# Criss-cross attention on one core: GpSimd's second subtractions of a position without their wait for VectorE's low halves

## The chip, the core and the metric

The kernel runs on one core of a Trainium2 chip. The metric is the time on the device of one execution in microseconds (us), lower is better. Before the change it is 3690.41 us, the median of 3 runs (3687.48 to 3691.53).

## The reference

For each of 8 images of 512 channels and 96 x 96 pixels, queries, keys and values are linear maps of the pixel's channels. Every pixel attends to the 96 pixels of its column (its own left out there) and the 96 of its row, with one softmax over both:

```python
q = jnp.einsum('oc,bchw->bohw', Wq, x) + bq[None, :, None, None]      # 64 channels
k = jnp.einsum('oc,bchw->bohw', Wk, x) + bk[None, :, None, None]
v = jnp.einsum('oc,bchw->bohw', Wv, x) + bv[None, :, None, None]      # 512 channels
energy_H = jnp.einsum('bchw,bcgw->bhwg', q, k) - NEG * eye[None, :, None, :]
energy_W = jnp.einsum('bchw,bchv->bhwv', q, k)
att = jax.nn.softmax(jnp.concatenate([energy_H, energy_W], axis=-1), axis=-1)
att_H, att_W = (att[..., :H], att[..., H:])
out_H = jnp.einsum('bcgw,bhwg->bchw', v, att_H)
out_W = jnp.einsum('bchv,bhwv->bchw', v, att_W)
return gamma * (out_H + out_W) + x
```

All is float32.

## The kernel before

The image is cut into 24 chunks (CHUNKS) of 4 rows (384 pixels). The attention weights are applied to x itself, by column and then by row, into Y, and only that sum is multiplied by the values' weights. Products that need more than one pass of TensorE are made with numbers split into a rounded high part and a low part, low = number - high. The high part is ScalarE's, the low part VectorE's or GpSimd's, and three matmuls (high x high, high x low, low x high) are summed in PSUM.

Each batch has a column stage and then a row stage of 24 positions n. In a position of the row stage TensorE

- multiplies the sums of chunk n by the values' weights (`project`, L1134, four groups of 12 matmuls),
- in positions 6 to 17 also makes queries and keys of two chunks of the next image (`project_kq`, L1032) and their row energies (`split_row_energies`, L1054),
- applies the attention to rows of chunk n + 2 (`attend_row`, L1122, four groups of 8 matmuls, in three PSUM banks that are used in turn, so that the fourth group needs the first one's sum moved out).

The next image's chunks in position n are a_now = [2(n - 6), 2(n - 6) + 1]: the first and the second half of the position. Positions 18 to 22 make the column energies instead. This happens in 7 of the 8 batches; in the last there is no next image.

Around the change:

- ScalarE: `round_kq` rounds keys and queries of a chunk (L602 and L603, the second signals kq_evicted). `round_y` makes the high parts of the sums of chunk n + 1 (L650, two halves), right behind the second `round_kq`. `copy_k` (L608) needs GpSimd's first subtraction. `row_exponentials` (L623, four per chunk) needs VectorE's maximum (L808). `round_x` is L579.
- VectorE: `finish` adds bias and input to a projected group (L881). `low_y` makes the low parts of the sums (L772, two halves, each signals y_lo_made). `add_row` takes a group of row sums out of PSUM (L872). `low_x` is L767. `add_energies` sums the energies' parts and takes their maximum (L805 twice, L808). Its order at the position's end is finish(2), finish(3), low_y half 0, add_row 0, low_y half 1, add_row 1, add_energies, add_row 2 and 3.
- GpSimd: `low_kq` makes the low parts of queries (L496) and keys (L499) of a chunk, once in each half of the position; `scale` (L477) multiplies attention weights by the softmax's factors.

Every engine runs its own list in the order in which it is written; semaphores tie the lists together. In positions 6 to 16 GpSimd has, in front of the second `low_kq`, a wait for both low halves of chunk n + 1. In position 17 (A_LAST) it has none.

Of the kernel before, what the change touches and what calls it, by code (L numbers as in the profile page):

```python
# [17 lines left out]
CHUNKS = N // ROWS  # L18
# [23 lines left out]
A_FIRST, A_LAST = 6, 17  # L42
# [4 lines left out]
def a_chunks(n):  # L47
    return [2 * (n - A_FIRST), 2 * (n - A_FIRST) + 1] if A_FIRST <= n <= A_LAST else []


def b_groups(n):
    first = (n - B_FIRST) * B_EACH
    return list(range(first, min(first + B_EACH, CHUNKS))) if B_FIRST <= n <= B_LAST else []
# [8 lines left out]
def criss_cross_attention(nc, x, x_col, x_row, wqk_t, wv_t, bqk, bv, gamma, out):  # L62
# [5 lines left out]
    HALVES = 2  # L68
# [6 lines left out]
    with ctx:  # L75
# [3 lines left out]
        def sem(name):  # L79
            return ctx.enter_context(nc.semaphore(name))  # L80
# [127 lines left out]
        y_hi_made, y_lo_made, y_half_used = sem("y_hi_made"), sem("y_lo_made"), sem("y_half_used")  # L208
# [12 lines left out]
        def past(s, n):  # L221
            return n + START[s]
# [220 lines left out]
        def _(pool):  # L443
# [3 lines left out]
            def gather_k(a, g):  # L447
                if g == 0:
                    pool.wait_ge(kq_evicted, past(kq_evicted, (a + 1) * CHUNKS))
                    pool.wait_ge(kg_zeroed, a + 1)  # L450
                pool.wait_ge(e_summed, past(e_summed, e_no(a, CHUNKS + g - 2)))
                src = KQ[0:CQ, :].rearrange("p (h w) -> p w h", w=N)[:, g * ROWS:(g + 1) * ROWS, :]
                nc.gpsimd.tensor_copy(Kg[0:CQ, g % 2, :].rearrange("p (w h) -> p w h", w=ROWS), src)\
                    .then_inc(k_gathered, 1)

            def zero_kg(a, before=True):
                if before:
                    out_landed(pool, a - 1, KG_SLOT)
                    pool.wait_ge(p_scaled, past(p_scaled, p_no(a - 1, CHUNKS + B_FIRST + 3)))
                nc.gpsimd.memset(Kg[CQ:P, :, :], 0.0).then_inc(kg_zeroed, 1)  # L460
                pool.wait_ge(kg_zeroed, a + 1)

            def mask(a, g):
                pool.wait_ge(e_exped, past(e_exped, e_no(a, CHUNKS + g)))
                at = by_block(E[0:N, g % ERING, :])
                nc.gpsimd.affine_select(out=at, in_=at, compare_op=ALU.not_equal, fill=0.0, base=0,
                                        pattern=[[-BLOCK, BLOCKS], [0, ROWS], [-1, BLOCK]], channel_multiplier=1)\
                    .then_inc(c_masked, 1)

            def scale(b, i):  # L470
                along, n = i // CHUNKS, i % CHUNKS
                if n == 0:
                    pool.wait_ge(f_made, past(f_made, b * 2 + along + 1))
                pool.wait_ge(p_in[p_buffer(i)], past(p_in[p_buffer(i)], 16 * p_loads(b, i)))
                f = F[:, along, :, n * ROWS:(n + 1) * ROWS].unsqueeze(3).to_broadcast((P, BLOCKS, ROWS, BLOCK))
                at = by_block(weights(i))
                nc.gpsimd.tensor_tensor(at, at, f, ALU.mult).then_inc(p_scaled, 1)  # L477
# [7 lines left out]
            def zero_q(a):  # L485
                pool.wait_ge(e_summed, past(e_summed, e_no(a, CHUNKS - 1)))
                nc.gpsimd.memset(Q[CQ:P, 1, :], 0.0).then_inc(q_zeroed, 1)
                pool.wait_ge(q_zeroed, a)

            def low_kq(a, m, last_scaled):  # L490
                pool.wait_ge(p_scaled, past(p_scaled, p_no(a - 1, last_scaled)))
                if m:
                    pool.wait_ge(kq_low_made, past(kq_low_made, split_no(a, m - 1) * 2))
                pool.wait_ge(kq_evicted, past(kq_evicted, a * CHUNKS + m + 1))
                at = slice(m * CP, (m + 1) * CP)
                nc.gpsimd.tensor_tensor(q_split[CQ:P, :], KQ[CQ:P, at], k_split[CQ:P, 0, :].bitcast(F32), ALU.subtract)\  # L496
                    .then_inc(kq_low_made, 1)
                pool.wait_ge(kq_low_made, past(kq_low_made, split_no(a, m) * 2 - 1))
                nc.gpsimd.tensor_tensor(k_split[0:CQ, 1, :], KQ[0:CQ, at], k_split[0:CQ, 0, :].bitcast(F32), ALU.subtract)\  # L499
                    .then_inc(kq_low_made, 1)  # L500

            def row_stage(b, more):
                scale(b, CHUNKS + 3)
                for n in range(CHUNKS):
                    a_now = a_chunks(n) if more else []
                    b_now = b_groups(n) if more else []
                    if a_now:
                        low_kq(b + 1, a_now[0], CHUNKS + n + 3)
                    if b_now and b_now[0] == 0:
                        zero_kg(b + 1)  # L510
                        gather_k(b + 1, 0)
                        gather_k(b + 1, 1)
                        zero_q(b + 1)
                    for g in b_now[:3]:
                        if g + 2 < CHUNKS:
                            gather_k(b + 1, g + 2)
                        mask(b + 1, g)
                    if n + 4 < CHUNKS:
                        scale(b, CHUNKS + n + 4)
                    if a_now:  # L520
                        if n < A_LAST:
                            pool.wait_ge(y_lo_made, past(y_lo_made, (b * CHUNKS + n + 2) * HALVES))
                        low_kq(b + 1, a_now[1], CHUNKS + n + 4)
                    for g in b_now[3:]:
                        if g + 2 < CHUNKS:
                            gather_k(b + 1, g + 2)
                        mask(b + 1, g)
# [21 lines left out]
            def whole(b):  # L549
                column_stage(b)  # L550
                row_stage(b, True)

            def last(b):
                column_stage(b)
                row_stage(b, False)
# [691 lines left out]
```

## Time and profile before

| | |
|---|---|
| median of 3 runs | 3690.41 us |
| profiled execution: time, span | 3688.54 us, 3686.8 us |
| granted TensorE clock, mean | 0.994 |
| TensorE busy | 3634.3 us, 99% |
| VectorE busy | 2677.8 us, 73% |
| ScalarE busy | 1867.5 us, 51% |
| GpSimd busy | 965.6 us, 26% |
| L772 (low parts of sums), VectorE | 384, mean 992 ns |
| L496, L499 (low parts of q and k), GpSimd | 168 each, mean 1008 and 1031 ns |

The span is from the first instruction to the last; the profiled execution's time is 1.7 us longer. Busy time is what an engine spends in instructions; its matmuls are pipelined and their ends modelled. In the traces PE is TensorE, DVE VectorE, ACT ScalarE and POOL GpSimd. In a timeline each row has the start in us from the span's start, the length in us, the engine, the line, the operation, out<-in, the shape and, in brackets, how long the engine had been idle before it and what ended that. On one engine an instruction's start can lie up to some 90 ns ahead of the end of the one before it. A granted clock of 1.00 is 2.4 GHz.

### The profile page before, as it was taken

The numbers are of one execution on the slowest core, as the hardware profiler recorded it, in microseconds if no ns is written. First come the engines' busy times: TensorE is split into PE (matmuls) and PEld (weight loads), VectorE is DVE, ScalarE is ACT, GpSimd is POOL, SyncE is SP. The second block draws the span as 40 slices with busy tenths as digits, with TensorE's granted clock in tenths as the row PEclk, the third lists the DMA queues.
The fourth block names the chain that finished last, engine by engine and source line by source line (L and its number), as shares of the span: only waits on it lengthen the run. The fifth ranks groups of instructions, "written<-read, shape, count | busy, mean of one in ns | idle before, by whom it ended". The sixth has DMA issues, their size and how long they took to land.

```text
span 3686.8 us, 67894 instructions
## 1 busy us (share of the span) xinstructions
PE 3634.3 (99%) x26296; PEld 3611.4 (98%) x26296; DVE 2677.8 (73%) x4326; ACT 1867.5 (51%) x3647; POOL 965.6 (26%) x1128
## 2 busy tenths in 40 slices
PE   8799999999999999999999999999999999999999
PEld 7799999999999999999999999999999999999999
DVE  7767787677876778767787677866778667786555
ACT  8525764257642676426754267542775427654111
POOL 1412243122431224202242022421224212342000
PEclk9899999999999999999999999999999999999999
DMA  8688868888698876977859787697776978769665
GB/s 273 171 237 259 267 199 244 230 269 261 196 250 238 262 259 195 257 238 260 261 176 269 236 264 256 181 266 242 257 250 199 263 242 258 237 207 256 210 208 181
DMA packets 333966, 874.01 MB, mean 237 GB/s; under 512 B 34640, under 2 KB 186704, under 8 KB 333648
## 3 DMA queue, kind: packets, MB, share of 16 engines
q1 hardware_dynamic: 333648, 869.67, 77.7%
q8 instruction: 211, 3.46, 0.4%
q14 instruction: 107, 0.88, 0.1%
HBM read 661.92 MB, written 207.62 MB: 236 GB/s over the span
## 4 chain that ended last, share of the span: by engine, by line
PE 96%; DVE 2%; issue 0%; DMA 0%; ACT 0%; POOL 0%; SPq 0%; DVEq 0%; ACTq 0%; POOLq 0%
PE bank L1134 44%; PE bank L1101 19%; PE bank L1122 18%; PE bank L1032 10%; PE bank L1068 3%; PE bank L1054 2%; DVE Sy L772 1%; DVE E L793 0%; PE bank L1086 0%; PE bank L1029 0%; PE bank L1042 0%; DMA e_scratch<-E 0%; DVE Y L872 0%; DVE mx_c L788 0%; ACT Sy L650 0%
## 5 line engine op out<-in xcount | busy, mean ns | idle before, releaser
L1134 PE MATMUL bank<-Sy,Wv_hi 128*128 128x384 f32 x6144 | 1588.6, 339 | 3.6 <-DVE Sy L772 3.6
L1134 PEld LDWEIGHTS bank<-Sy,Wv_hi 128*128 128x128 f32 x6144 | 1090.1, 189 | 7.2 <-issue 4.8
L1134 PE MATMUL bank<-Sy,Wv_lo 128*128 128x384 f32 x3072 | 1030.6, 335 | 0.0
L881 DVE SCALAR_TENSOR_TENSOR Y<-bank,bv_sb,Y 128x384 f32<-128x384 f32 x768 | 466.3, 612 | 405.4 <-PE bank L1134 404.4
L1122 PE MATMUL bank<-Pt,XT 128*128 128x96 f32 x6144 | 717.3, 274 | 0.3
L1122 PEld LDWEIGHTS bank<-Pt,XT 128*128 128x128 f32 x6144 | 713.7, 192 | 1.6 <-DVE Y L872 1.5
L1101 PE MATMUL bank<-Pt,XT 128*128 128x96 f32 x6144 | 690.4, 276 | 1.0 <-issue 1.0
L1101 PEld LDWEIGHTS bank<-Pt,XT 128*128 128x128 f32 x6144 | 689.6, 193 | 1.2 <-issue 1.2
L650 ACT ACTIVATE Sy<-Y 128x768 fp32r<-128x768 f32 x384 | 311.9, 838 | 687.1 <-PE bank L1134 649.2
L1134 PEld LDWEIGHTS bank<-Sy,Wv_lo 128*128 128x128 f32 x3072 | 579.0, 188 | 0.0
L477 POOL TENSOR_TENSOR Pe<-Pe,F 128x384 f32<-128x384 f32 x336 | 279.8, 835 | 1076.9 <-DMA Pe<-e_scratch 1041.5
L767 DVE TENSOR_TENSOR Sx<-XA,Sx 128x768 fp32r<-128x768 f32 x348 | 334.3, 964 | 291.1 <-ACT Sx L579 291.1
L637 ACT ACTIVATE Y<-bank 128x384 f32<-128x384 f32 x384 | 327.0, 852 | 416.6 <-PE bank L1101 416.6
L865 DVE COPY Y<-bank 128x384 f32<-128x384 f32 x384 | 317.6, 828 | 200.0 <-PE bank L1101 180.3
L496 POOL TENSOR_TENSOR q_split<-KQ,k_split 64x384 fp32r<-64x384 f32 x168 | 169.3, 1008 | 1051.8 <-DVE Sy L772 553.0
L872 DVE TENSOR_TENSOR Y<-bank,Y 128x384 f32<-128x384 f32 x768 | 400.2, 547 | 9.1 <-PE bank L1122 8.9
L772 DVE TENSOR_TENSOR Sy<-Y,Sy 128x768 fp32r<-128x768 f32 x384 | 380.9, 992 | 5.1 <-ACT Sy L650 5.1
L1032 PE MATMUL bank<-Sx,Wqk_hi 128*128 128x384 f32 x1416 | 368.5, 341 | 10.0 <-DVE Sx L767 10.0
L623 ACT ACTIVATE E<-E,mx_r 96x96 f32<-96x96 f32 x672 | 243.7, 364 | 172.1 <-DVE mx_r L808 171.9
L579 ACT ACTIVATE Sx<-XA 128x768 fp32r<-128x768 f32 x348 | 288.1, 832 | 41.9 <-PE bank L1032 31.5
L1032 PEld LDWEIGHTS bank<-Sx,Wqk_hi 128*128 128x128 f32 x1416 | 250.8, 189 | 10.3 <-issue 10.3
L859 DVE STREAM_TRANSPOSE Pt<-Pe 128x384 f32<-128x384 f32 x336 | 234.9, 699 | 29.4 <-PE bank L1101 4.2
(83 smaller groups left out, 3122.6 us busy)
## 6 DMA issues: line engine op xcount, KB each, us to landing
XT<-in_x_col SPq DMA_DIRECT2D x384, 384.0 KB, 5.7
XT<-in_x_row SPq DMA_DIRECT2D x384, 384.0 KB, 5.9
Y<-in_x SPq DMA_DIRECT2D x192, 768.0 KB, 6.6
out<-Y SPq DMA_DIRECT2D x184, 768.0 KB, 4.4
XA<-in_x SPq DMA_DIRECT2D x180, 768.0 KB, 5.0
e_scratch<-E SPq DMA_DIRECT2D x384, 144.0 KB, 3.0
Pe<-e_scratch SPq DMA_DIRECT2D x336, 144.0 KB, 5.4
XA_first<-in_x SPq DMA_DIRECT2D x12, 768.0 KB, 6.3
```

Source lines behind the costliest of these rows:

```text
L579: nc.scalar.activation(sx(a, m)[:, 0, cts, :], xa(a, m)[:, cts, :], ACT.Copy).then_inc(x_hi_made, 1)
L637: nc.scalar.activation(to, oc_ps[i % CBANKS][:, 0:CT * N].rearrange("p (t n r) -> p t n r", t=CT, r=ROWS), ACT.Copy).then_inc(c_moved_act, 1)
L650: nc.scalar.activation(Sy[:, 0, cts, :], Y[:, n + 1, cts, :], ACT.Copy).then_inc(y_hi_made, 1)
L767: nc.vector.tensor_tensor(sx(a, m)[:, 1, cts, :], xa(a, m)[:, cts, :], sx(a, m)[:, 0, cts, :].bitcast(F32), ALU.subtract).then_inc(x_lo_ma ...
L772: nc.vector.tensor_tensor(Sy[:, 1, halves[h], :], Y[:, n + 1, halves[h], :], Sy[:, 0, halves[h], :].bitcast(F32), ALU.subtract).then_inc(y ...
L865: nc.vector.tensor_copy(to, oc_ps[i % CBANKS][:, 0:CT * N].rearrange("p (t n r) -> p t n r", t=CT, r=ROWS))\
L872: nc.vector.tensor_tensor(at, or_ps[i % RBANKS][:, 0:CT * N].rearrange("p (t n) -> p t n", t=CT), at, ALU.add).then_inc(r_added, 1)
L881: nc.vector.scalar_tensor_tensor(at, proj_ps[c % 2][:, 0:CP], bv_sb[:, c:c + 1], at, op0=ALU.add, op1=ALU.add).then_inc(out_made, 1)
L1032: last = nc.tensor.matmul(ps[:, 0:CP], w[:, ct, :], sx(a, m)[:, lo, ct, :], start=(ct == 0 and n == 0), stop=(ct == CT - 1 and n == 2))
L1101: last = nc.tensor.matmul(oc_ps[i % CBANKS][:, ct * N:(ct + 1) * N], XT[:, j % XRING, u, ct * P:(ct + 1) * P], Pt[:, g % 2, r * N:(r + 1) ...
L1122: last = nc.tensor.matmul(or_ps[i % RBANKS][:, ct * N:(ct + 1) * N], XT[:, j % XRING, u, ct * P:(ct + 1) * P], Pt[:, n % 2, r * N:(r + 1) ...
L1134: last = nc.tensor.matmul(proj_ps[c % 2][:, 0:CP], w[:, ct, at], Sy[:, lo, ct, :], start=(ct == 0 and k == 0), stop=(ct == CT - 1 and k == 2))
```

## The change

In GpSimd's row stage, in the second half of a position, the wait for y_lo_made is taken out:

```diff
                     if a_now:
-                        if n < A_LAST:
-                            pool.wait_ge(y_lo_made, past(y_lo_made, (b * CHUNKS + n + 2) * HALVES))
                         low_kq(b + 1, a_now[1], CHUNKS + n + 4)
```

The waits inside `low_kq` stay: for the last `scale` (p_scaled), for its own last subtraction (kq_low_made) and for kq_evicted. No instruction is added, removed or moved on any engine, and no DMA is touched; 77 waits go, one in each of 11 positions of 7 batches.

## Rows read from the trace of the kernel before

**Rows 1.** The page: busy us (share of the span) and instructions of each engine:

```profile
PE 3634.3 (99%) x26296; PEld 3611.4 (98%) x26296; DVE 2677.8 (73%) x4326; ACT 1867.5 (51%) x3647; POOL 965.6 (26%) x1128
```

**Rows 2.** Stretch of position 8: length, busy PE, PEld, DVE, ACT, POOL, granted clock, DMA, GB/s:

```profile
351.37:368.18 16.81, 16.81 (x114) 16.78 (x113) 13.05 (x22) 12.02 (x31) 4.82 (x5) 1.00 0.82 261
```

**Rows 3.** Waits: engine, line, waited for: us in total, times, longest:

```profile
POOL q_split L496 <- DVE Sy L772: 553.0, 77, 8.0
```

**Rows 4.** Timeline of GpSimd, position 8: start, us, engine line operation, idle before:

```profile
354.46 1.00 POOL L496 TENSOR_TENSOR q_split<-KQ,k_split 64x384 fp32r<-64x384 f32 x1 [7.14 <-DVE Sy L772]
```

**Rows 5.** Timeline of ScalarE, position 8 to 9:

```profile
350.58 0.58 ACT L603 ACTIVATE q_split<-bank,bqk_sb 64x384 fp32r<-64x384 f32 x1
...
356.39 0.38 ACT L623 ACTIVATE E<-E,mx_r 96x96 f32<-96x96 f32 x1 [0.38 <-DVE mx_r L808]
...
362.60 0.38 ACT L623 ACTIVATE E<-E,mx_r 96x96 f32<-96x96 f32 x1 [1.53 <-DVE mx_r L808]
...
367.39 0.58 ACT L603 ACTIVATE q_split<-bank,bqk_sb 64x384 fp32r<-64x384 f32 x1
```

**Rows 6.** Timeline of ScalarE, position 17:

```profile
501.38 0.58 ACT L603 ACTIVATE q_split<-bank,bqk_sb 64x384 fp32r<-64x384 f32 x1
```

**Rows 7.** Timeline of GpSimd, position 17:

```profile
502.12 1.01 POOL L496 TENSOR_TENSOR q_split<-KQ,k_split 64x384 fp32r<-64x384 f32 x1 [3.47 <-ACT q_split L603]
503.21 0.99 POOL L499 TENSOR_TENSOR k_split<-KQ,k_split 64x384 fp32r<-64x384 f32 x1
```

**Rows 8.** Timeline of VectorE, position 8 to 9:

```profile
352.10 0.95 DVE L772 TENSOR_TENSOR Sy<-Y,Sy 128x768 fp32r<-128x768 f32 x1
352.97 0.55 DVE L872 TENSOR_TENSOR Y<-bank,Y 128x384 f32<-128x384 f32 x1
353.44 0.95 DVE L772 TENSOR_TENSOR Sy<-Y,Sy 128x768 fp32r<-128x768 f32 x1
...
358.70 0.96 DVE L767 TENSOR_TENSOR Sx<-XA,Sx 128x768 fp32r<-128x768 f32 x1 [1.42 <-ACT Sx L579]
...
367.81 1.19 DVE L881 SCALAR_TENSOR_TENSOR Y<-bank,bv_sb,Y 128x384 f32<-128x384 f32 x2
```

**Rows 9.** Timeline of VectorE, first half of position 6:

```profile
309.77 1.73 DVE L767 TENSOR_TENSOR Sx<-XA,Sx 128x768 fp32r<-128x768 f32 x1
311.43 0.61 DVE L881 SCALAR_TENSOR_TENSOR Y<-bank,bv_sb,Y 128x384 f32<-128x384 f32 x1
311.95 0.69 DVE L859 STREAM_TRANSPOSE Pt<-Pe 128x384 f32<-128x384 f32 x1
```

**Rows 10.** Timeline of GpSimd, the same stretch:

```profile
309.68 1.01 POOL L496 TENSOR_TENSOR q_split<-KQ,k_split 64x384 fp32r<-64x384 f32 x1 [15.12 <-ACT q_split L603]
310.76 1.62 POOL L499 TENSOR_TENSOR k_split<-KQ,k_split 64x384 fp32r<-64x384 f32 x1
```

**Rows 11.** Timeline of VectorE, position 17:

```profile
503.42 1.60 DVE L772 TENSOR_TENSOR Sy<-Y,Sy 128x768 fp32r<-128x768 f32 x1
504.94 0.54 DVE L872 TENSOR_TENSOR Y<-bank,Y 128x384 f32<-128x384 f32 x1
```

**Rows 12.** Timeline of TensorE, attention matmuls of positions 6, 8 and 17:

```profile
317.74 3.48 PE L1122 MATMUL bank<-Pt,XT 128*128 128x96 f32 x30
...
351.37 3.71 PE L1122 MATMUL bank<-Pt,XT 128*128 128x96 f32 x32
...
502.69 3.99 PE L1122 MATMUL bank<-Pt,XT 128*128 128x96 f32 x32
```

**Rows 13.** Timeline of ScalarE, position 6:

```profile
316.43 0.58 ACT L603 ACTIVATE q_split<-bank,bqk_sb 64x384 fp32r<-64x384 f32 x1
```

**Rows 14.** Waits: TensorE for VectorE, at the end of position 17:

```profile
PE bank L1054 <- DVE E L805: 11.6, 7, 1.7
```

**Rows 15.** Stretches after two stalls of TensorE; columns as in rows 2:

```profile
508.00:512.00 4.00, 3.59 (x14) 3.62 (x15) 3.22 (x7) 3.07 (x13) 1.28 (x2) 0.61 0.74 246
583.00:587.00 4.00, 3.64 (x24) 3.32 (x23) 3.67 (x8) 1.23 (x3) 0.95 (x1) 1.00 1.03 268
```

## The prediction

> **What bounds the kernel now.** I read the page's busy line first: TensorE is busy 3634.3 us, 99% of the span [rows 1]. Then the stretch of one position in the middle of the edited ones, in the table of stretches: TensorE is busy 16.81 us of 16.81 at a granted clock of 1.00 [rows 2]. So in the edited positions there is nothing to win: whatever the edit frees, TensorE has no idle time there to give back. The list of waits shows what the edit touches: GpSimd's L496 waits 553.0 us for VectorE's L772 (the low halves of the sums), 77 times, which is 11 positions (6 to 16) of 7 batches [rows 3]. No name in that row is TensorE's. The question is only what GpSimd's work will lie beside once it comes earlier.
>
> **What is removed, and where the work goes.** No instruction goes or comes, and none changes places on its engine. In position 8 of batch 0 (TensorE starts its 32 attention matmuls at 351.37) L496 starts at 354.46, after 7.14 us of waiting [rows 4]. What remains to wait for is ScalarE's L603, which ends at 350.58 + 0.58 = 351.16 [rows 5]. In position 17, where the wait was never there, L603 ends at 501.38 + 0.58 = 501.96 and L496 starts at 502.12, 0.16 later [rows 6, 7]. So L496 will run from 351.32 to about 352.32 (1.00 long [rows 4]), and L499 wants to follow at 352.40.
>
> There VectorE makes the low halves: L772 at 352.10, an add of a row (L872) at 352.97, and L772 again at 353.44, 0.95 us each [rows 8]. L772, like L496 and L499, reads two operands from SBUF. What such a pair does to each other is shown in the first half of position 6, where they meet already: L496 runs 309.68 to 310.69 [rows 10]; VectorE's L767 (a subtraction of the same shape) is ready at 309.77 and takes 1.73 instead of 0.96 [rows 8], so it ends at 311.50, 0.81 after L496 let go [rows 9]. L499 began at 310.76, behind the waiting L767, and takes 1.62 instead of 1.00: it ends at 312.38, 0.88 after L767 [rows 10]. They don't slow each other, they take turns, and the one that already waits is next. The Trainium skill (SBUF — State Buffer, Who interferes with whom) states this as an exclusive lock between a VectorE instruction with two SBUF inputs and a GpSimd instruction that reads SBUF, where the issue order decides who blocks; the rows agree, with 0.81 and 0.88 us left to run after the other's end, nearly a whole turn. By that rule the sum is the one below; were the port's rate only divided between the two, VectorE would lose less than 0.43 us per position and the total would lie between 3690 and 3720.
>
> **One position, step by step.** L496 until 352.32. First L772 ready at 352.10, ends 352.32 + 0.81 = 353.13 (now 353.05). L499 gets the next turn, ends 353.13 + 0.88 = 354.01. The add of a row between them has one operand in PSUM; I count it as undisturbed, as VectorE's L881 beside the running L499 is at 0.61 us, also with one operand in PSUM [rows 9]. Second L772 ready at 353.5, blocked to 354.01, ends 354.01 + 0.81 = 354.82, against 353.44 + 0.95 = 354.39 now: 0.43 us later.
>
> **Is there slack to take up 0.43 us?** This is the step that decides. I follow what comes behind the second L772. VectorE goes on without a pause to L808; ScalarE's exponentials start at 356.39, having waited 0.38 us for just that L808, and L579 follows [rows 5]. VectorE's L767 at 358.70 had waited 1.42 us for that L579 [rows 8], and so on in turns to VectorE's pair of L881 at 367.81 and ScalarE's L603 at 367.39, ending 367.97 [rows 5, 8]. That is 351.16 + 16.81. The idle spots of both engines in it are waits for each other; it is a loop, of ScalarE and VectorE, which is as long as TensorE's position. TensorE's own hold on it is the second L881 of the pair: the two together take 1.19 us, against 0.52 + 0.61 = 1.13 for two that follow with no wait (an estimate from one L881 that the next instruction follows after 311.95 - 311.43 = 0.52, and its length 0.61 [rows 9]), so the slack is about 0.05 us. The new path avoids even that: it runs from L603's end over L496, L772, L499, L772. From there: 351.16 to 354.82 is 3.66, 354.39 to 367.97 is 13.58, together 17.24 us against TensorE's 16.81 [rows 2]. From both sides: a gain per position is excluded, since TensorE is already full; at least 0 would be left if the loop hid more slack than the rows show, at most 1.16 if GpSimd kept the pair from L496 over into L499 (rival 3). I take 0.43, since the first half of position 6 has the same GpSimd instructions and the same order of arrival [rows 9, 10].
>
> **When TensorE feels it.** The first to be missed is the add of the row that frees the PSUM bank of the position's fourth attention group. In position 8 it ends 352.97 + 0.55 - 351.37 = 2.15 us after the start of the 32 matmuls. In position 17 it ends 504.94 + 0.54 - 502.69 = 2.79 after, and the 32 take 3.99 instead of 3.71 us, 0.28 more [rows 11, 12]. So TensorE needs it by 2.51, and there is 0.36 us of cover now, 0.27 once the first L772 is 0.09 later.
>
> **The sum of a batch.** Second half of position 6: L603 ends at 316.43 + 0.58 = 317.01, 0.73 before the attention start at 317.74 [rows 12, 13], as in position 17 (501.96 against 502.69). There L499, from 503.21, comes before L772, which takes 1.60 instead of 0.95 [rows 7, 11]: 0.65 us lost for the loop, and the same 0.28 of TensorE. The loop leaves it 0.65 - 0.28 = 0.37 behind TensorE. Position 7: stall 0.37 - 0.27 = 0.10. From position 8 to 16 the cover is used up, and each costs the whole 0.43: 9 x 0.43 = 3.87. Position 17 is as before: ScalarE and VectorE have less to do in 16 and 17 and meet TensorE again. Together 0.28 + 0.10 + 3.87 = 4.25 us per batch, and 7 x 4.25 = 30 us (29.8). Where exactly TensorE is caught matters little: without any cover it were 7 x 0.27 = 2 us more, with 1 us of it 5 us less.
>
> What ScalarE gains: L608 can run earlier with L496, by 354.46 - 351.32 = 3.1 us, but the exponentials behind it wait for L808 anyway [rows 5], so it is worth nothing.
>
> Profiled execution: 3688.5 + 30 = 3718.5 us; the median shown, 3690.4, lies 1.9 above it: 3720 us, 0.8% slower. Its own range: growth per position between 0.33 and 0.50 gives 23 to 35 us.
>
> **Rivals.**
> 1. VectorE gets the pair again ahead of L499 for its second L772. Then only 0.09 per position is lost, of which 0.05 is slack: after position 6 nearly nothing grows, 0.28 + 0.10 + 0.3 per batch, 5 us, 3695 us. For it: nothing in the rows. Against: the turn that L499 took there [rows 10], though what followed on VectorE there was an L881, which doesn't ask for the pair. 6%.
> 2. Not slower: the loop has slack which the profile hides (an instruction of the chain that starts early as soon as it can), so that 0.43 per position is absorbed between L808 and L603. It decides once that slack is over 0.43 us; the time is then 3690 us. For it: ScalarE idles 1.53 us in the middle of the loop, VectorE 1.42 [rows 5, 8]. Against: each of these idle spots ends with the other engine's instruction, so they are part of the loop's length. 6%. A real gain would have to come from the only wait of TensorE near the edit, L1054 for L805, 11.6 us in all at the end of position 17 [rows 14], if the earlier L608 fed into it: at most 3679 us. That wait is for VectorE's sums, on which the edit has no hold. 2%.
> 3. GpSimd keeps the pair from L496 to L499. The first L772 ends 352.32 + 0.08 + 1.00 + 0.81 = 354.21, 1.16 later than now, and the second, unblocked, as much. Position 7 then stalls 0.37 + 1.16 - 0.36 = 1.17, and a batch costs 0.28 + 1.17 + 9 x 1.16 = 11.9 us, all seven 83, 3773 us. Against: in the first half of position 6 the waiting VectorE got in between [rows 9, 10]. 5%.
> 4. The stalls bring the clock down. After the 1.7 us stall of position 17 the granted clock is 0.61 over 508 to 512, a share of that stretch at 1.2 instead of 2.4 GHz [rows 15]: about 0.39 x 4 = 1.6 us. Were that so at each of 77 stalls it would cost 120 us, 3840 us. Against: over 583 to 587 TensorE is idle for 4.00 - 3.64 = 0.36 us and its clock stays at 1.00 [rows 15], and my stalls are of that size. 2%.
>
> **How the numbers follow.** Forecast 79%, rivals 6, 6 + 2, 5 and 2%. The range 3706 to 3734 us leaves out the first two rivals below and the last two above, and takes in most of the forecast's spread. A measurement of this kernel can tell 0.2%, 7 us, from no change: slower by more is the forecast, rivals 3 and 4 and a little of the first (88%), within it the rest of rivals 1 and 2 (10%), faster 2%.
>
> **What would show it.** In the profile after: the wait of L496 for L772 is gone; in positions 8 to 16 the position's period is 17.2 instead of 16.81 us; L772's mean is above 1.0 us (one half about 1.03 long, the other about 1.3 to 1.4), L499 about 0.6 longer in those positions; TensorE waits before the last eight of the 32 attention matmuls, for L872, by about 0.4 us; L496, L805, L808, L872 and ScalarE's operations keep their lengths; the column stage, positions 0 to 5 and 18 to 23 and the last batch stay as they are. I am wrong if the period stays 16.81 with L772 longer (slack I didn't see), or if the L772 are not lengthened (no turns taken).

## The result and the profile after

| | before | after |
|---|---|---|
| median, 5 runs each | 3688.78 us | 3720.82 us |
| lowest to highest | 3687.05 to 3691.53 us | 3718.24 to 3720.96 us |
| span of the profiled execution | 3686.8 us | 3719.1 us |

The ratio is 1.0084, with a 95% interval of 1.0069 to 1.0099: 0.8% slower, about 32 us. (In the code after, the lines behind the change count two less: L770 is L772 of before, L601 is L603, L806 is L808, L1030 is L1032.)

Waits of the profile after, which answer to [rows 3]: engine, line, what ended the wait, us in total, times, longest.

```profile
POOL q_split L496 <- ACT q_split L601: 1043.8, 168, 16.6
ACT E L621 <- DVE mx_r L806: 418.5, 161, 4.1
PEld bank L1030 <- ACT q_split L601: 29.7, 71, 0.4
```

GpSimd waits for no low half any more. ScalarE's exponentials wait 418.5 us for VectorE's maximum, where they had waited 171.9: the time that L608 freed on ScalarE went straight into that wait (L608's own wait for L496 fell from 220.8 to 8.3 us). And TensorE has a wait that it didn't have: its weight loads (PEld) for the queries and keys, 71 times.

The stretches (length, busy us of PE, PEld, DVE, ACT, POOL, then granted clock, DMA share, GB/s), after: positions 6 to 16 of batch 0, positions 8 and 9 alone, and position 17.

```profile
318.14:507.84 189.70, 188.63 (x1234) 184.91 (x1233) 146.80 (x229) 130.91 (x329) 58.91 (x56) 1.00 0.75 245
352.57:369.81 17.24, 17.14 (x113) 16.79 (x113) 13.46 (x23) 12.01 (x31) 5.41 (x5) 1.00 0.80 255
369.81:387.07 17.26, 17.16 (x114) 16.81 (x114) 13.48 (x23) 12.03 (x31) 5.41 (x5) 1.00 0.79 255
507.84:525.50 17.66, 16.40 (x110) 16.06 (x109) 14.36 (x25) 10.80 (x28) 8.87 (x12) 0.90 0.58 177
```

and the first and the last of them in the kernel before:

```profile
317.74:502.69 184.95, 184.95 (x1234) 184.68 (x1234) 141.72 (x229) 130.90 (x329) 53.58 (x56) 1.00 0.77 252
502.69:520.86 18.17, 16.39 (x110) 16.05 (x109) 14.88 (x25) 10.79 (x28) 8.15 (x12) 0.91 0.53 171
```

A position takes 17.25 us where it took 16.81 [rows 2]; VectorE is busy 13.46 instead of 13.05 and GpSimd 5.41 instead of 4.82 us with the same instructions, at the same clock. The eleven positions are 4.75 us longer.

The timeline of VectorE in position 8 after, against [rows 8], and of GpSimd beside it, against [rows 4]:

```profile
352.50 1.14 DVE L879 SCALAR_TENSOR_TENSOR Y<-bank,bv_sb,Y 128x384 f32<-128x384 f32 x2
353.56 1.09 DVE L770 TENSOR_TENSOR Sy<-Y,Sy 128x768 fp32r<-128x768 f32 x1
354.57 0.55 DVE L870 TENSOR_TENSOR Y<-bank,Y 128x384 f32<-128x384 f32 x1
355.04 1.28 DVE L770 TENSOR_TENSOR Sy<-Y,Sy 128x768 fp32r<-128x768 f32 x1
356.24 0.54 DVE L870 TENSOR_TENSOR Y<-bank,Y 128x384 f32<-128x384 f32 x1
356.71 1.00 DVE L803 TENSOR_REDUCE E<-bank 96x192 f32<-96x384 f32 x2
```

```profile
352.83 1.01 POOL L496 TENSOR_TENSOR q_split<-KQ,k_split 64x384 fp32r<-64x384 f32 x1 [3.99 <-ACT q_split L601]
353.91 1.59 POOL L499 TENSOR_TENSOR k_split<-KQ,k_split 64x384 fp32r<-64x384 f32 x1
```

L496 ends at 353.84, and the first L770, ready at 353.56, ends at 354.65, 0.81 later. L499 ends at 355.50, 0.85 after that. The second L770 ends at 356.32, 0.82 after L499. They take turns, in the order that the prediction gave. L496, L803 and L870 keep their lengths.

TensorE in the same position: the 32 attention matmuls, and the one weight load that waits.

```profile
352.57 3.74 PE L1120 MATMUL bank<-Pt,XT 128*128 128x96 f32 x32
```

```profile
363.06 0.30 PEld L1030 LDWEIGHTS bank<-Sx,Wqk_hi 128*128 128x128 f32 x2 [0.42 <-ACT q_split L601]
```

Only 0.03 us of the loss is in the attention matmuls (3.74 against 3.71 [rows 12]). The rest comes about seven microseconds after their end, where TensorE starts the second chunk's queries and keys and needs their one PSUM bank, which ScalarE's L601 (362.43 + 0.58 = 363.01) has just emptied. (The profile shows such a matmul as 0.34 us long where the next normally starts 0.17 us later. That hides part of a late start, and PE is still called busy for 17.14 us of the 17.24; the period shows the loss, the busy share doesn't.)

### The profile page after: what moved, and what is told of

Its sections match the earlier page's. It is cut to its first block, busy times and chain, and to the rows that moved or that the text cites. A ratio compares the mean times of both kernels' runs of the same rounds, so it can differ in the third digit from the quotient of the medians.

```text
span 3719.1 us, 67817 instructions
## 1 busy us (share of the span) xinstructions
PE 3656.3 (98%) x26296; PEld 3608.6 (97%) x26296; DVE 2713.7 (73%) x4326; ACT 1867.8 (50%) x3647; POOL 1007.2 (27%) x1128
## 4 chain that ended last, share of the span: by engine, by line
PE 72%; DVE 13%; ACT 11%; issue 2%; DMA 1%; POOL 0%; SPq 0%; ACTq 0%; DVEq 0%; POOLq 0%
PE bank L1132 30%; PE bank L1099 18%; PE bank L1120 14%; PE bank L1030 6%; ACT Sx L577 4%; ACT E L621 4%; DVE Sy L770 3%; PE bank L1066 3%; DVE E L803 2%; DVE Sx L765 2%; DVE Y L879 2%; DVE Y L870 1%; ACT KQ L593 1%; DVE mx_r L806 1%; DMA e_scratch<-E 1%
## 5 line engine op out<-in xcount | busy, mean ns | idle before, releaser
L621 ACT ACTIVATE E<-E,mx_r 96x96 f32<-96x96 f32 x672 | 244.3, 365 | 418.7 <-DVE mx_r L806 418.5
L496 POOL TENSOR_TENSOR q_split<-KQ,k_split 64x384 fp32r<-64x384 f32 x168 | 169.4, 1008 | 1043.8 <-ACT q_split L601 1043.8
L770 DVE TENSOR_TENSOR Sy<-Y,Sy 128x768 fp32r<-128x768 f32 x384 | 418.8, 1091 | 5.1 <-ACT Sy L648 5.1
L870 DVE TENSOR_TENSOR Y<-bank,Y 128x384 f32<-128x384 f32 x768 | 399.6, 547 | 9.0 <-PE bank L1120 8.5
L1030 PE MATMUL bank<-Sx,Wqk_hi 128*128 128x384 f32 x1416 | 378.2, 348 | 16.7 <-DVE Sx L765 9.7
L1030 PEld LDWEIGHTS bank<-Sx,Wqk_hi 128*128 128x128 f32 x1416 | 247.0, 189 | 40.0 <-ACT q_split L601 29.7
```

Of the source, the lines that this page charges most:

```text
L621: last = nc.scalar.activation(row, row, ACT.Exp, bias=mx_r[:, at], accum_out=zs_r[:, at])
L770: nc.vector.tensor_tensor(Sy[:, 1, halves[h], :], Y[:, n + 1, halves[h], :], Sy[:, 0, halves[h], :].bitcast(F32), ALU.subtract).then_inc(y ...
L870: nc.vector.tensor_tensor(at, or_ps[i % RBANKS][:, 0:CT * N].rearrange("p (t n) -> p t n", t=CT), at, ALU.add).then_inc(r_added, 1)
L1030: last = nc.tensor.matmul(ps[:, 0:CP], w[:, ct, :], sx(a, m)[:, lo, ct, :], start=(ct == 0 and n == 0), stop=(ct == CT - 1 and n == 2))
```

## The experiments

Each time is the median of 4 to 11 runs, each ratio (with its 95% interval) is to runs of the kernel before on the same chip. In some of their kernels the line numbers are 1 to 5 higher than before; the same operation is meant.

### Wait for the first half only

```diff
-  pool.wait_ge(y_lo_made, past(y_lo_made, (b * CHUNKS + n + 2) * HALVES))
+  pool.wait_ge(y_lo_made, past(y_lo_made, (b * CHUNKS + n + 2) * HALVES - 1))
```

> In positions 6 to 16 GpSimd's second subtractions wait for the first low half of the sums only, so they start about 1.3 us earlier than in the kernel before and 1.8 us later than in the changed one. Theory A (VectorE and GpSimd take turns on instructions with two SBUF operands, and the loop of ScalarE and VectorE has no slack): L496 starts as the first L772 ends (353.12 on the clock of position 8), the second L772 waits for its end at 354.12 and ends at 354.93, 0.54 later than before; of that 0.05 is slack. 11 x 0.49, less about 0.3 of cover, is 5.1 us per batch, 36 us in all: 3725 us, more than the changed kernel although a wait is left. Theory B (the cost grows with how much earlier GpSimd's work comes, by whatever cause): between the two kernels, about 3700 us.

Measured: 3722.17 us, ratio 1.0091 (1.0077 to 1.0104), 33 us. The stretch of position 8, then VectorE and GpSimd in it:

```profile
351.80:369.17 17.37, 17.11 (x113) 16.77 (x113) 13.59 (x23) 12.05 (x31) 5.42 (x5) 1.00 0.78 253
```

```profile
352.82 0.96 DVE L772 TENSOR_TENSOR Sy<-Y,Sy 128x768 fp32r<-128x768 f32 x1
353.70 0.55 DVE L872 TENSOR_TENSOR Y<-bank,Y 128x384 f32<-128x384 f32 x1
354.16 1.50 DVE L772 TENSOR_TENSOR Sy<-Y,Sy 128x768 fp32r<-128x768 f32 x1
```

```profile
353.86 1.00 POOL L496 TENSOR_TENSOR q_split<-KQ,k_split 64x384 fp32r<-64x384 f32 x1 [5.78 <-DVE Sy L772]
354.93 1.61 POOL L499 TENSOR_TENSOR k_split<-KQ,k_split 64x384 fp32r<-64x384 f32 x1
```

The first half is free, the second has to wait for L496 (354.86) and takes 1.50 us, while L496 keeps its 1.00 us beside the waiting VectorE: the one that runs isn't slowed. The positions last 17.35 us, 0.54 more than before. Half of the protection does nothing for the time, as theory A has it; theory B is out. That the total exceeds the changed kernel's is told by the positions (5.6 us per batch against 4.8), not by the totals, whose intervals overlap.

### Only the keys wait

Made from the changed kernel; `low_y_of` is given in the second half of positions 6 to 16 and is None elsewhere. The wait stands between L496 and L499:

```diff
                 pool.wait_ge(kq_low_made, past(kq_low_made, split_no(a, m) * 2 - 1))
+                if low_y_of is not None:
+                    pool.wait_ge(y_lo_made, past(y_lo_made, low_y_of * HALVES))
```

> In positions 6 to 16 the second subtraction of the queries (L496) is free, that of the keys (L499) waits for both low halves of the sums. Theory A: only the first L772 is held up, by 0.11 us, the second not at all. 10 positions x 0.11, less about 0.4 of cover, is 0.7 us per batch, 5 us in all: 3694 us. Theory B (what costs is that the queries' low part and with it ScalarE's copy of k, L608, come early): the time of the changed kernel, 3720 us.

Measured: 3691.83 us, ratio 1.0010 (1.0002 to 1.0019), about 3 us. L608 comes early here as in the changed kernel, and nearly nothing is lost. In the trace positions 6 to 8 last 16.81 us, and from position 10 or 11 on about 16.92: the 0.11 us grows unseen until the cover is used up, and then each position pays it. Positions 8 and 12:

```profile
351.60:368.41 16.81, 16.81 (x114) 16.79 (x113) 13.04 (x22) 11.94 (x30) 4.82 (x5) 1.00 0.82 261
419.07:435.99 16.92, 16.92 (x114) 16.80 (x113) 13.16 (x23) 12.03 (x31) 4.82 (x5) 1.00 0.80 260
```

### Nothing to read

In the changed kernel, the second low_kq of positions 6 to 16 is two memsets of the same outputs:

```diff
+                if m % 2 and m // 2 + A_FIRST < A_LAST:
+                    nc.gpsimd.memset(q_split[CQ:P, :].bitcast(F32), 0.0).then_inc(kq_low_made, 1)
+                    pool.wait_ge(kq_low_made, past(kq_low_made, split_no(a, m) * 2 - 1))
+                    nc.gpsimd.memset(k_split[0:CQ, 1, :].bitcast(F32), 0.0).then_inc(kq_low_made, 1)
+                    return
```

> As the changed kernel, but the second pair of subtractions in positions 6 to 16 is replaced by two memsets of the same outputs: the low parts of queries and keys of every second chunk are left out (zero). The memsets read nothing. Theory A: no turns to take with VectorE, both L772 stay at 0.95 us, period 16.81 us, 3689 us (plus or minus 3). Theory B (the missing wait itself, or the early L608, costs): 3720 us.

Measured: 3687.28 us, ratio 0.9997 (0.9988 to 1.0006). Without the wait, at the same place, and nothing is lost. GpSimd's groups of the 77 pairs (count, busy us, mean ns, idle before):

```profile
L497 POOL MEMSET q_split<- 64x384 f32 x77 | 31.8, 413 | 306.9 <-ACT q_split L606 306.9
L499 POOL MEMSET k_split<- 64x384 f32 x77 | 31.7, 411 | 4.4
```

Positions 8 and 9 last 16.81 us. So the missing wait and the early L608 cost nothing by themselves. The memsets are also shorter (0.41 us each) and are mostly over when the first low half starts, so the time of this run doesn't part reading from length. In one of the 77 pairs, where GpSimd came later, the second memset lies almost wholly beside the low half, and neither is held up. VectorE and GpSimd there:

```profile
854.43 0.95 DVE L775 TENSOR_TENSOR Sy<-Y,Sy 128x768 fp32r<-128x768 f32 x1
```

```profile
854.39 0.41 POOL L499 MEMSET k_split<- 64x384 f32 x1
```

That is a single case, but it is what one would see if only reading makes them take turns.

### The loop without GpSimd's part

The kernel before, its wait in place, with one more reduction on VectorE in each of positions 6 to 16:

```diff
                 dve.wait_ge(e_added, past(e_added, split_no(a, m) * 2))
+                if m % 2 == 0 and m // 2 + A_FIRST < A_LAST:
+                    nc.vector.tensor_reduce(spare[:, :], to, AX_XY, ALU.max, negate=True)
```

> The kernel before, with one more maximum (as L808, 0.47 us from start to start, written to a tile that nobody reads) on VectorE ahead of the first chunk's in positions 6 to 16; GpSimd untouched. Theory A's second step (the loop of ScalarE and VectorE has 0.05 us of slack): 0.42 us per position, 11 positions less 0.3 us of cover, 4.3 us per batch, 30 us: 3719 us, period 17.23 us. Rival (the loop has slack, and only GpSimd's part in it costs): 3689 us.

Measured: 3716.14 us, ratio 1.0076 (1.0063 to 1.0088), 27 us. Positions 8 and 9 of it:

```profile
350.44:367.66 17.22, 17.09 (x113) 16.75 (x113) 13.45 (x24) 12.00 (x31) 4.83 (x5) 1.00 0.79 255
367.66:384.92 17.26, 17.11 (x113) 16.77 (x113) 13.49 (x24) 12.04 (x31) 4.83 (x5) 1.00 0.80 255
```

VectorE is 73% busy over the span, and 0.47 us more of it in a position costs 0.43. This shows the second step by itself: the loop of ScalarE and VectorE is as long as TensorE's position, to within some 0.05 us, and GpSimd's part is not needed to lengthen it. Here too TensorE waits at L1032's counterpart for ScalarE (33.7 us, 77 times).

### Every second position

The kernel before, with the wait left in the even positions alone:

```diff
-                        if n < A_LAST:
+                        if n < A_LAST and n % 2 == 0:
```

> The wait is taken out in positions 7, 9, 11, 13 and 15 alone and stays in the even ones. Theory A (the loop has no slack, a loss is kept until cover is used up): each of the five adds 0.44 us, the cover of about 0.48 us is paid once, an even position gives nothing back: periods of 16.81, 16.81, then 17.2 in the odd ones from about 9 on and 16.81 in the even ones; 1.7 us per batch, 12 us in all: 3701 us. Rival (each loss is made good in the next position, so that the changed kernel pays only because the losses follow each other without a break): 3689 us.

Measured: 3695.61 us, ratio 1.0014 (1.0005 to 1.0023), 5 us: less than half of what was expected. The positions do what theory A says. Positions 8 and 9, and then 17:

```profile
350.68:367.52 16.84, 16.84 (x114) 16.82 (x113) 13.07 (x23) 12.08 (x31) 4.82 (x5) 1.00 0.83 261
367.52:384.72 17.20, 17.11 (x114) 16.76 (x113) 13.43 (x22) 11.97 (x31) 5.41 (x5) 1.00 0.79 256
503.65:519.45 15.80, 14.61 (x110) 14.40 (x110) 13.95 (x25) 10.82 (x28) 9.15 (x12) 1.00 0.64 198
```

Positions 6 to 16 are 1.8 us longer in most batches (1.7 expected) and 13.0 us longer in all seven together, with nothing made good in the even ones. What I had left out is position 17: there the seven batches take 117.0 us together in this trace and 123.6 in the trace before. That is the stall of [rows 14] and the fall of the clock behind it [rows 15]. A fall adds about 1.5 us to the position; the trace before has one in five of the seven batches, this one has one. The two parts give 13.0 - 6.6 = 6.4 us, and the spans differ by 6.3.

### Position 17

Three kernels leave 6 to 16 as they were and change position 17 alone. First, the wait is put there too:

```diff
-                        if n < A_LAST:
+                        if n <= A_LAST:
```

> The wait of positions 6 to 16 is added in position 17 as well. Theory A: both L772 there take 0.95 instead of 1.60 and 1.46 us, but L499 now ends 5.2 us after the start of the attention matmuls and TensorE's L1054 needs it: L1054 starts at 5.25 instead of 5.72. 7 x 0.47 = 3 us less: 3686 us. If the clock falls after fewer of the seven stalls, up to 1.5 us less for each. Rival (the late subtractions and gathers of GpSimd cost more than VectorE gains): 3690 us or more.

Second, only the keys' subtraction waits, and only in position 17 (`low_y_of` is None elsewhere):

```diff
                 pool.wait_ge(kq_low_made, past(kq_low_made, split_no(a, m) * 2 - 1))
+                if low_y_of is not None:
+                    pool.wait_ge(y_lo_made, past(y_lo_made, low_y_of * HALVES))
```

> The kernel before, and in position 17 the second L499 waits for both low halves, L496 for none. Theory A: neither L772 is held up there, L805 of the last but one chunk ends about 4.4 us after the start of the attention matmuls, L1054 starts at 4.5 instead of 5.72: 7 x 1.2 = 8.6 us less, 3680 us; with stalls of 0.8 instead of 1.7 us, if the clock stays up after them, another 1.5 us for each of about five batches, down to 3673 us. Rival (L1054 is held by something else at 5.7): 3689 us.

Third, VectorE's order, with the keys waiting for the first half alone (`low_y_of * HALVES - 1`):

```diff
                         add_row(b, n + 2, 0)
+                        if n == A_LAST and a_now:
+                            add_energies(b + 1, a_now[0])
                         low_y(b, n + 1, 1)
                         add_row(b, n + 2, 1)
-                        if a_now:
+                        if n < A_LAST and a_now:
                             add_energies(b + 1, a_now[0])
```

> Position 17 alone is changed: VectorE sums the energies of the last but one chunk between the first row add and the second low half, and GpSimd's second L499 waits for the first low half only. Theory A: L805 ends at about 3.1 us after the start of the attention matmuls, L1054 follows them without a stall, the second low half is done at 4.5 to 5.2 us and just in time: 7 x 2.0 = 14 us less and no clock lost after a stall (about 1.5 us in five of seven batches): 3667 us. Rival (the second low half comes too late and TensorE waits for it instead): 3680 us or more.

Measured: 3681.59 us (0.9978, 0.9969 to 0.9987), 3673.94 us (0.9957, 0.9944 to 0.9969) and 3673.55 us (0.9956, 0.9943 to 0.9968). TensorE's waits there, one row from each in this order (L1057 is L1054 of before, L1073 is L1068, and in both of the last two L808 is the sum L805, not the maximum):

```profile
PE bank L1054 <- POOL k_split L499: 10.9, 7, 1.6
```

```profile
PE bank L1057 <- DVE E L808: 5.9, 7, 0.8
```

```profile
PE bank L1073 <- DVE E L808: 5.7, 7, 0.8
```

With the full wait the stall stays, now for GpSimd: L1054 starts 5.26 us after the attention matmuls' start, as expected, and the stall is 1.55 us. The clock falls in two batches of this trace instead of five, and so the gain is about 9 us and not the 3. With the keys alone the stall is halved and no fall is left in the seven positions 17. The third was 7 us off: the stall at L1054 is gone, as expected, but the same sum of the chunk after it is now late for L1068's counterpart, 0.8 us again. So, as one more step from this third kernel (the next two texts call it e8, and the kernel made from it e9):

```diff
+                        if more and n == A_LAST:
+                            add_energies(b + 1, a_now[1])
                         add_row(b, n + 2, 2)
                         add_row(b, n + 2, 3)
-                    if more and n == A_LAST:
-                        add_energies(b + 1, a_now[1])
```

> As e8_sums_first_in_17, and VectorE sums the last chunk's energies ahead of the last two row adds of position 17, not behind them. In e8 TensorE's L1073 waits 0.82 us for that sum in each of seven batches. Theory A: L805 of the last chunk ends 5.9 us after the start of the attention matmuls instead of 6.85, TensorE's wait is gone: 7 x 0.8 = 5.7 us less than e8, 3668 us. Rival (L1073 then waits for GpSimd's gather of k, which comes at about the same time): 3672 us.

Measured: 3666.81 us, ratio 0.9942 (0.9930 to 0.9955), 22.6 us faster than the kernel before. Position 17 has no stall:

```profile
500.95:515.47 14.52, 14.52 (x109) 14.31 (x109) 13.53 (x25) 10.82 (x28) 8.73 (x12) 1.00 0.70 214
```

### The change on a kernel without that stall

Made from the last kernel, in which the wait stands as in the kernel before:

```diff
-                        if n < A_LAST:
-                            pool.wait_ge(y_lo_made, past(y_lo_made, (b * CHUNKS + n + 2) * HALVES))
```

> As e9_both_sums_first_in_17, and without the wait of positions 6 to 16 (the change under study, on a kernel whose position 17 has no stall of TensorE and no fall of the clock behind it). Theory A: the change costs what positions 6 to 16 show, 4.8 us per batch, 34 us in all, a little more than the 31 to 32 us seen on the kernel as it was, where position 17 happened to be 3 us cheaper: 3702 us if e9 is at 3668. Rival (position 17 hides or adds nothing): 31 us, 3699 us.

Measured: 3701.41 us, 34.6 us above the kernel that it is made from (3666.81); the spans of the profiled executions differ by 36.5.

```profile
317.39:507.29 189.90, 188.71 (x1233) 184.98 (x1233) 146.80 (x229) 131.21 (x329) 58.96 (x56) 1.00 0.75 245
507.29:521.79 14.50, 14.50 (x109) 14.29 (x109) 13.53 (x25) 10.85 (x28) 8.43 (x12) 1.00 0.69 215
```

Positions 6 to 16 cost 189.90 - 184.94 = 5.0 us in this batch, 34.5 us in all seven, and position 17 is the same in both: the change costs about 34 us by itself. (The other 2 us between the two spans lie elsewhere, 1.4 of them before the first row stage.) On the kernel before, the trace shows 33.9 us in positions 6 to 16, and position 17 is 3.1 us cheaper after the change (120.5 against 123.6 us for seven batches), with three falls of the clock instead of five. The spans differ by 32.3 us; the 1.5 us left over lie in single delays of at most 0.6 us at the start and around the column stages, which the edit doesn't touch, and stay unexplained. The other executions point the same way: the mean granted clock is 0.995 or 0.996 in all five after the change and 0.993 to 0.995 in the 52 of the kernel before that ran beside the experiments. But that mean also counts falls near the start, so how many fewer there usually are in position 17 is not shown, nor why.

## Why the prediction was right

**Where GpSimd's work goes, and the turns**: right, to a few hundredths. L496 followed L601 by 0.17 us (expected 0.16), L770 took 1.09 and 1.28 us (expected 1.03 and 1.3 to 1.4), L499 1.59 (1.61). The memsets and the first-half wait agree. A rate divided between the two, the other reading that the prediction names without a chance of its own, is out: L496 keeps 1.01 us here and 1.00 beside a VectorE that waits 0.70 us for it in the first experiment.

**No slack in the loop**: right, and the step on which all rests. The period was to be 17.24 us and is 17.25. The extra maximum shows the loop without the turns, the keys' wait shows a loss of 0.11 us per position kept and paid later, and the alternate positions show that nothing is given back in between. The slack of 0.05 us, read from how closely two instructions followed each other, fits too: 0.43 us of 0.47 for the extra maximum.

**When TensorE feels it**: right in size, wrong in place. I named the row add and its PSUM bank, with 0.36 us of cover. In position 6 TensorE does wait there, and the 32 matmuls take 3.99 us as forecast. But the second project_kq waits too, and from position 7 on it is the one that waits, 0.42 us at the weight load. Its cover could be read from the trace of before, which I hadn't done for this consumer. ScalarE's L603 of the position's first half, and TensorE's weight load that needs it, in position 8:

```profile
360.50 0.58 ACT L603 ACTIVATE q_split<-bank,bqk_sb 64x384 fp32r<-64x384 f32 x1
```

```profile
361.39 0.36 PEld L1032 LDWEIGHTS bank<-Sx,Wqk_hi 128*128 128x128 f32 x2
```

L603 ends 9.71 us after the attention start and the weight load starts at 10.02 (its matmul at 10.19), so the cover is 0.31 us. That accounts for position 6: the loop is 0.65 us late there, as forecast, 0.31 of it is covered, and the position is 17.15 - 16.81 = 0.34 us longer, where the attention matmuls alone gave 0.28. As argued beforehand, the place hardly matters once the loop is the longer one. It matters in position 7: 0.10 us was expected, and 17.28 - 16.81 = 0.47 measured, since both covers are gone by then. The experiments were forecast with a cover of 0.3 to 0.48 us; 0.31 fits what they measured. With the extra maximum, position 6 is 0.14 us longer and not 0.44; with alternate waits, position 7 is 0.13 longer and not 0.44; with the keys' wait alone, 0.11 us per position stays unseen for three positions.

**The sum**: 4.25 us per batch against 4.75 in the first batch and 4.8 over the seven (33.9 us in all). Short by 0.4 in position 7 and a little in the others (0.06 in position 6); then 3.1 us too much in position 17, which I took as unchanged. The two errors have opposite signs, and the total, 30 us forecast and 32 measured, owes some of its closeness to that.

**Rivals**: VectorE doesn't get a second turn ahead of L499 (1), the loop absorbs nothing and an earlier L608 wins nothing (2), GpSimd doesn't keep the pair (3). The stalls of 0.4 us don't bring the clock down (4): it is 1.00 over positions 6 to 16. The clock rival was looked for at the wrong place; it acts behind the 1.7 us stall of position 17, where the change shifts only how often.

## What to carry to other kernels

An engine that is 73% busy can still have no slack: follow the chain from one of its instructions through the other engines back to it one period later, and if every idle spot ends with a member of the chain, its length is a second bound beside the busiest engine's. A wait that holds up only an idle engine may be what keeps that engine's reads out of the chain. Look for the place where such a wait is missing, too: here spacing the same instructions in the one position that had none, and summing first what TensorE needs first, gave 0.6%.

## What was not expected of the hardware

The clock's fall behind a stall of 1.7 us does not come every time. In the kernel before, position 17 with the same stall lasts 18.2 us in five batches (granted clock 0.91 over it) and in another of the same trace 16.6 (clock 1.00); the seventh has a stall of 1.2 us and no fall, 16.1 us. A stall of 1.2 us can see one as well: that is the 17.66 us at a clock of 0.90 in the rows of the result. In the seven traces whose position 17 was left as it was (before, after and the first five experiments) the clock falls behind 19 of 42 stalls of 1.7 us and 2 of 7 of 1.2 us. In the others it falls behind two of seven of 1.55 us and none of fourteen of 0.8. So a change elsewhere in the program can win or lose some microseconds there without touching it: 6.6 us in the kernel with alternate waits.
